# Comparing the gates in PSUM, with the copy to SBUF behind the comparisons

## The reference, cut to what matters

```
gate = sigmoid((token_inputs @ Wg)[..., 0])          # one number per token, 512 per sequence
_, idx = top_k(gate, 256)                            # the half of the tokens with the largest gates
attn_in = take_along_axis(token_inputs, idx)         # 256 x 256
o = attention(attn_in; Wq, Wk, Wv, Wo), 16 heads     # over the chosen tokens only
out = zeros; out[idx] = o * gate[idx]                # back to the places of the tokens
```

## Time and profile before

| | us |
|---|---|
| median of three runs | 2163.89 |
| the profiled execution, as timed | 2163.86 |
| its span, first to last instruction | 2162.1 |
| PE busy | 2077.1 (96% of the span) |
| DVE busy | 1438.5 (67%) |
| ACT busy | 1094.0 (51%) |
| POOL busy | 562.8 (26%) |

### The profile page before, as it was taken

How to read it: one execution, slowest core, us unless ns; L and a number is a source line. 1 busy time by engine, 2 the same in 40 slices (tenths; PEclk the granted TensorE clock), 3 DMA queues, 4 the chain that set the end, 5 groups by cost and what they waited for, 6 DMA issues and landing times.

```text
span 2162.1 us, 38720 instructions
## 1 busy us (share of the span) xinstructions
PE 2077.1 (96%) x14694; PEld 1276.1 (59%) x14694; DVE 1438.5 (67%) x4530; ACT 1094.0 (51%) x2465; POOL 562.8 (26%) x785
## 2 busy tenths in 40 slices
PE   7889999999999999999999999999999999999997
PEld 4456566654666555764566645766456664666665
DVE  8876554667756776567656587575875767756435
ACT  2344573646536474363744646346563646526552
POOL 4311231243212331133311332114230233202220
PEclk9999999999999999999999999999999999999999
DMA  3001121121111110121101111011110121101200
GB/s 139 2 1 40 42 90 40 54 74 33 43 40 54 57 42 27 40 72 47 39 22 57 62 40 42 18 57 62 40 59 1 57 69 50 43 16 57 68 18 10
DMA packets 29047, 98.56 MB, mean 46 GB/s; under 512 B 2880, under 2 KB 11200, under 8 KB 28736
## 3 DMA queue, kind: packets, MB, share of 16 engines
q1 hardware_dynamic: 28864, 96.09, 13.3%
HBM read 91.89 MB, written 4.19 MB: 44 GB/s over the span
## 4 chain that ended last, share of the span: by engine, by line
PE 86%; DVE 7%; ACT 5%; issue 1%; POOL 1%; DMA 0%; SPq 0%; DVEq 0%; POOLq 0%; ACTq 0%
PE ps L845 25%; PE ps L1498 11%; PE ps L1508 11%; PE ps L1490 10%; PE ps L1283 10%; PE ps L1340 4%; PE ps L1429 3%; PE ps L1360 3%; PE ps L1374 3%; PE ps L1460 2%; PE ps L1448 2%; ACT PTc L1029 2%; DVE ps L1148 2%; DVE mcol L1224 1%; ACT probs L1061 1%; DVE probs L1241 1%
## 5 line engine op out<-in xcount | busy, mean ns | idle before, releaser
L993 POOL TENSOR_SCALAR probs<-probs,rtotal 128x512 f32<-128x512 f32 x512 | 345.1, 697 | 1022.5 <-DVE rtotal L1250 1021.4
L1061 ACT ACTIVATE probs<-probs,peak 128x512 f32<-128x512 f32 x512 | 365.2, 714 | 238.8 <-DVE peak L1246 238.7
L1241 DVE CUSTOM_DVE_ANT_0 probs<-ps,band 128x512 f32<-128x512 f32 x512 | 332.8, 687 | 134.1 <-PE ps L1490 133.8
L1070 ACT ACTIVATE PT<-ps 128x512 f32<-128x512 f32 x512 | 263.7, 612 | 74.4 <-PE ps L1498 72.8
L1148 DVE CUSTOM_DVE_ANT_0 ps<-ps,later 128x128 f32<-128x128 f32 (+3 forms) x512 | 233.1, 525 | 39.7 <-PE ps L1340 38.8
L1498 PEld LDWEIGHTS ps<-ident,probs 128*128 128x128 f32 x2048 | 224.0, 141 | 47.5 <-issue 31.5
L1498 PE MATMUL ps<-ident,probs 128*128 128x128 f32 x2048 | 250.1, 275 | 0.5 <-POOL probs L993 0.2
L1490 PE MATMUL ps<-KT,QT 64*128 64x512 f32 x1024 | 249.0, 611 | 0.0
L1508 PE MATMUL ps<-PT,Vb 128*64 128x512 f32 x1024 | 235.4, 599 | 0.5 <-ACT PT L1070 0.5
L845 PE MATMUL ps<-xnT,wb 128*128 128x512 f32 x512 | 234.6, 597 | 0.8 <-ACT xnT L1012 0.3
L1029 ACT ACTIVATE PTc<-ps 128x384 f32<-128x384 f32 (+1 forms) x384 | 166.3, 543 | 69.6 <-PE ps L1360 69.6
(11 more groups left out here) (125 smaller groups left out, 2808.5 us busy)
## 6 DMA issues: line engine op xcount, KB each, us to landing
band<-in_band SPq DMA_DIRECT2D x64, 896.0 KB, 4.5
wb<-in_w_b SPq DMA_DIRECT2D x64, 384.0 KB, 3.1
x<-in_x SPq DMA_DIRECT2D x16, 256.0 KB, 3.0
out<-x SPq DMA_DIRECT2D x16, 256.0 KB, 2.3
wob<-in_wo_b SPq DMA_DIRECT2D x1, 1024.0 KB, 8.3
wqk<-in_wqk_a SPq DMA_DIRECT2D x1, 512.0 KB, 5.6
cos_t<-in_cos SPq DMA_DIRECT2D x1, 256.0 KB, 5.4
sin_t<-in_sin SPq DMA_DIRECT2D x1, 256.0 KB, 6.0
```

Source lines behind the costliest of these rows:

```text
L993: last = g.tensor_scalar(unit, unit, rtotal[:, r % 8, e:e + 1], 1.0, ALU.mult, ALU.mult)
L1061: last = a.activation(unit, unit, ACT.Exp, bias=peak[:, r % 8, e:e + 1], accum_out=total[:, r % 8, e:e + 1])
L1070: a.activation(PT[:, k % 2, e, :, tile_of(q)], bank(now, name).rearrange("p (k n) -> p k n", k=NT), ACT.Copy).then_inc(act_read, 1)
L1241: v.tensor_tensor_reduce(out=probs[:, r % ROWS_HELD, e, :], in0=bank(now, name), in1=band[:, k % 2, e, lo:lo + T], scale=1.0, scalar=-3e38 ...
```

## The change: what it does

The comparisons in `f_row` take their first operand from the PSUM bank itself, and the copy to `gate_row` is issued as the last of the twelve DVE instructions. The wait between copy and comparisons goes. `above_done` is raised by the last comparison as before, so ahead of the copy; `dve_read`, which frees the bank, is raised by the copy, so now at the end. The rest of the kernel is the same.

```diff
@@ -1183,19 +1183,19 @@
                         if kind == "f_row":
                             at_least(dve, consts, CONSTS)
-                            v.tensor_copy(m.gate_row[:], bank(now)).then_inc(dve_read, 1)
-                            dve.wait_ge(dve_read, plan.unit(now, now))
+                            row = bank(now)
                             for t in range(NT):
-                                v.scalar_tensor_tensor(out=m.tie[:, t, :], in0=m.gate_row[:, tile_of(t)],
+                                v.scalar_tensor_tensor(out=m.tie[:, t, :], in0=row[:, tile_of(t)],
                                                        scalar=m.gate[:, t:t + 1], in1=before[:], op0=ALU.is_equal,
                                                        op1=ALU.mult)
                             for t in range(NT):
-                                last = v.tensor_scalar(m.above[:, t, 0:(t + 1) * P], m.gate_row[:, 0:(t + 1) * P],
+                                last = v.tensor_scalar(m.above[:, t, 0:(t + 1) * P], row[:, 0:(t + 1) * P],
                                                        m.gate[:, t:t + 1], None, ALU.is_lt)
                                 if t < NT - 1:
-                                    v.tensor_scalar(m.above[:, t, (t + 1) * P:T], m.gate_row[:, (t + 1) * P:T],
+                                    v.tensor_scalar(m.above[:, t, (t + 1) * P:T], row[:, (t + 1) * P:T],
                                                     m.gate[:, t:t + 1], None, ALU.is_le)
                             last.then_inc(above_done, 1)
+                            v.tensor_copy(m.gate_row[:], row).then_inc(dve_read, 1)
```

## The result

The changed kernel takes 2174.7 us (median of four runs, 2172.05 to 2177.43), the kernel before 2163.57 beside it. The two medians lie 11.1 us apart; the ratio given with the runs is 1.0045, its 95% interval 1.0033 to 1.0057, which is 9.7 us more (7.1 to 12.3). So the changed kernel is slower. The forecast was 2173.8. The profiled execution took 2174.67 us, its span is 2172.9.

The account below looks back on a forecast made before the run. PE bounds the kernel (busy 96%, 86% of the chain), so DVE time counts only where PE waits for it. The places, 5.5 + 2.6 + 0.6 + 0.9 + 0.3 = 9.9 us, give 2173.8 us, range 2165.5 to 2180.

Parts of the forecast that it names:

- part 3: Seven comparisons of `above` cost 1.03 ns a column from PSUM, not 0.52: 1.04 us more, bounds -0.4 or +0.45 a step.
- The rival of the fast rate: Comparisons keep 0.52 ns a column in PSUM, so the time is 2163, not slower; chance 5%.
- the fixed price for reading PSUM: Rival: each of the eleven comparisons pays more to begin in PSUM, 64 ns each, giving 2185; chance 5%.
- parts 1 and 4: Copy and its wait leave the head of DVE's step (0.73 us less); the copy at the tail adds 0.61.
- part 5: The PSUM bank is held 4.76 us after the step starts instead of 0.69, yet is free in time: costs 0.
- Kind A: Six places where DVE's picks and PE reach the gather together, without slack: 0.92 us each, 5.5 in all.
- Kind B: Seven places where DVE idle time and slack before the gather absorb part of the delay: 0.37 each, 2.6 in all.
- Sequence 6, first and last layer: The three other places: 0.6 us, partly absorbed by DVE idle time; 0.9, no DVE gap; 0.3, copy hidden behind ranks.
- Given back later: Rival: PE's new waits let other engines run ahead, so its next waits shorten; time 2168.5, chance 18%.

Follow-up runs that it names:

- held: Kernel before, copy first and comparisons from SBUF, with only the bank's release moved from the copy to the last comparison; 2164.01 us, ratio 1.0001.
- more_work: Kernel before plus two more 512-column comparisons from SBUF into a scratch tile that nothing reads; 2170.82 us, ratio 1.0038.
- copy_head: Changed kernel with the copy issued first, no wait behind it, and the bank released by the last comparison; 2175.25 us, ratio 1.0058.
- a_only: Kernel before with the changed form only in layer 1 of sequences 2 to 7, the six places of Kind A; 2168.95 us, ratio 1.0033.
- after_b: The changed kernel run again without any diff, in five rounds; median 2172.8 us, ratio 1.0052.
- last_only: Kernel before with the changed form only in the last gated layer (sequence 7, layer 3); 2165.46 us, ratio 1.0004.

## Why the prediction was right, step by step

- **The rate of the comparisons in PSUM (part 3).** Forecast 1.03 ns a column and 740 ns for 512; measured 1.04 and 742. The bounds on both sides weren't needed. The rival of the fast rate falls. So does the fixed price for reading PSUM: 344 ns for a tie against 348, and what a comparison costs besides its columns is 742 - 512 x 1.04 = 209 ns where it was 214. The Trainium skill, page "VectorE: DVE Perf Modes", section "The TRN2 errata — SBUF-src ops pay a fixed extra latency per instruction", gives 120 cycles of start from PSUM against 58 from SBUF; that difference does not show in these two forms.
- **The length of the step (parts 1 and 4).** Forecast +0.92; measured 4.65 - 3.76 = +0.89. The copy costs 0.60 at the tail.
- **The held bank (part 5).** Forecast nothing; held shows nothing.
- **Kind A.** Forecast 6 x 0.92 = 5.5; measured 6 x 0.89 = 5.3. That DVE time and nothing else does it is shown by more_work and copy_head; a_only, with no other place changed, came out 6.1 above its before, its interval 4.3 to 9.7.
- **Kind B.** Forecast 0.37 each, 2.6; measured 0.33 to 0.35 in six of them. The seventh, at 190.66, does not look as the earlier trace rows, as the prediction had it: four projection matmuls and the four of one more bias row stand ahead of its ranks on PE, it takes 14.85 us from step to gather and lengthens by 0.31. From start to start the seven give 2.3.
- **Sequence 6, first and last layer.** Forecast 0.6, 0.9, 0.3; measured 0.53 (177.15 against 176.62 from this step to the last), 0.99 (84.21 against 83.22 from the first step to the second; with the low stretches of the clock in it, other kernels with this layer changed took 83.72 to 86.89) and 0.33 to the gather.
- **Given back later.** None of it: the period grew by 1.23 (262.71 against 261.48), the sum of a place of kind A and one of kind B.

So the sum of the places is 9.5 where 9.9 was forecast, and 9.7 was timed by the ratio (10.0 by the medians of after_b, 11.1 by those of the first series). The mechanism and its sizes are shown by the places. That the timed value is so near is in part luck: the interval is 2.6 us to either side. The term that the prediction did not have is the clock: PE ran at the lower level for some stretches ahead of the first step and behind the last, at other times in every execution. In the two profiled executions it goes with most of what the spans differ by outside the steps, -2.15 at one end and some +3.5 at the other. These two have opposite signs, which is part of why the spans' 10.8 comes near the count's 9.5.

## What to carry to other kernels

In this kernel a read of PSUM in place of SBUF was free for the three-operand compare, which costs 1.03 ns a column from either, and doubled the column price of the one-input compare in fp32, 0.52 ns from SBUF and 1.04 from PSUM; so look up both rows before a copy is taken away from in front of several readers. Then count the whole queue of the engine, not the instruction that raises the signal: here the signal came 0.3 us later but the queue behind it 0.9, and the queue is what the next wait of PE hung on. Where the copy has to stay, the operations that cost the same in PSUM can run behind it and cover the wait for its result.

## What the runs showed of the hardware

The time lost at the clock's lower level moved about between executions of one kernel: the same 16 matmuls took 3.72 us at the full clock and 6.1 to 6.3 at a mean granted clock of 0.58 to 0.60, in kernels with and without a change nearby (5.4 in last_only, where the lower level covered only part of them). In before the lower level fell at the start of the last layer on the 20 transposes that only fill PE's time: they took 4.01 us, where they took 2.35 in the changed kernel, and that cost nothing. The nine executions of the changed kernel spread from 2171.7 to 2178.2 us. A DVE copy of 512 columns from PSUM took 680 ns directly behind another DVE instruction (the changed kernel), and 692 where DVE had waited for the bank (before).
